# Low splits of the expert weights: from two engines in whole pieces to one engine in half pieces

## The reference

```
scores  = softmax(xt @ Wg.T)                   # 1024 tokens, 16 experts
combine = weights of the 4 experts of a token (from the 2 best groups of 4)
h       = silu(xt @ W1[e].T) * (xt @ W3[e].T)  # 176 wide
y       = sum over e of combine[:, e] * (h @ W2[e].T)
z       = silu(xt @ Ws1.T) * (xt @ Ws3.T) @ Ws2.T     # the shared expert, 352 wide
out     = x + y + z
```

## Time and profile before

| what | us |
|---|---|
| median of 3 runs (635.8 to 640.08) | 636.93 |
| the profiled execution | 642.02 |
| its span, first to last instruction | 640.6 |
| mean granted clock of TensorE | 0.961 of full |

### The profile page before, as it was taken

One profiled execution on the slowest core, in us unless ns is written; L12 is line 12 of the kernel. 1 busy time (PEld: TensorE's weight loads), 2 busy tenths in 40 slices (PEclk: granted clock), 3 DMA queues, 4 the chain that ended last, 5 costly groups with the idle time before them and its releaser, 6 DMA issues.

```text
span 640.6 us, 10499 instructions
## 1 busy us (share of the span) xinstructions
PE 569.4 (89%) x3751; PEld 470.4 (73%) x3751; DVE 391.3 (61%) x906; ACT 249.2 (39%) x515; POOL 211.5 (33%) x174
## 2 busy tenths in 40 slices
PE   6889999999999979999999998998889688999950
PEld 6668888898888978566566575676779477999940
DVE  3475765628356467866647655787656667555527
ACT  1334535535464351010312111236332477566630
POOL 3624540021000011322343332316165469444440
PEclk9889999999999999999999999999797898999985
DMA  8999904004030036996000000222061483334317
GB/s 246 265 237 226 202 14 165 1 1 180 12 113 2 1 116 222 336 331 223 1 0 1 1 1 1 111 118 76 17 231 67 119 283 91 108 112 128 115 37 293
DMA packets 25121, 76.93 MB, mean 120 GB/s; under 512 B 4839, under 2 KB 11631, under 8 KB 24432
## 3 DMA queue, kind: packets, MB, share of 16 engines
q1 hardware_dynamic: 19264, 62.33, 32.5%
q0 software_dynamic: 3792, 8.43, 3.7%
q10 hardware_dynamic: 2016, 5.50, 2.7%
HBM read 66.77 MB, written 28.48 MB: 149 GB/s over the span
## 4 chain that ended last, share of the span: by engine, by line
PE 58%; DVE 15%; issue 10%; DMA 7%; POOL 5%; ACT 3%; another core or an unknown queue 1%; SPq 1%; ACTq 0%; POOLq 0%; DVEq 0%
PE psum L684 8%; PE psum L702 6%; PE psum L853 5%; PE psum L553 5%; PE psum L618 5%; PE psum L605 5%; DMA sclB<-in_scl 5%; PE psum L566 4%; DVE tt L1254 3%; DVE Pb L1218 2%; PE psum L746 2%; POOL rows_of_experts L1631 2%; DMA yv<-parts_of_tokens 2%; PE psum L597 2%; PE psum L584 1%
## 5 line engine op out<-in xcount | busy, mean ns | idle before, releaser
L1254 DVE TENSOR_TENSOR tt<-psum,tab 128x512 f32<-128x512 f32 x96 | 60.8, 683 | 32.4 <-PE psum L684 31.9
L1603 POOL TENSOR_TENSOR rp<-tt,tt 128x512 f32<-128x512 f32 x24 | 30.7, 1278 | 106.1 <-DVE tt L1254 106.1
L553 PE MATMUL psum<-xTh,W 128*128 128x512 f32 x128 | 53.7, 419 | 8.4 <-DVE W L1154 6.6
L702 PE MATMUL psum<-rp,Mb 128*128 128x512 f32 x128 | 57.7, 595 | 0.3 <-DVE rp L1279 0.3
L853 PE MATMUL psum<-EW,xgh 128*128 x188 | 57.4, 347 | 0.4 <-issue 0.4
L1224 DVE TENSOR_TENSOR OTl<-psum,OTh 128x512 fp32r<-128x512 f32 x32 | 22.1, 692 | 53.9 <-ACT OTh L954 53.9
L553 PE MATMUL psum<-xTl,W 128*128 128x512 f32 x128 | 52.4, 410 | 0.0
L1637 POOL DMA_INDIRECT parts_of_tokens<-yb,xg x39 | 41.2, 1056 | 33.6 <-issue 26.7
L987 ACT ACTIVATE qP<-psum 128x512 f32<-128x512 f32 x16 | 9.6, 598 | 94.7 <-PE psum L702 94.7
L684 PE MATMUL psum<-xTh,Ah 128*128 128x512 f32 x96 | 41.9, 436 | 4.4 <-DVE ex_la L1334 2.3
L702 PEld LDWEIGHTS psum<-rp,Mb 128*128 128x128 f32 x128 | 23.7, 189 | 26.4 <-issue 25.7
(11 more groups left out here) (254 smaller groups left out, 1550.7 us busy)
## 6 DMA issues: line engine op xcount, KB each, us to landing
rows_of_experts<-in_empty SPq DMA_DIRECT2D x8, 2064.0 KB, 33.2
exr<-in_ex SPq DMA_DIRECT2D x9, 608.0 KB, 6.5
xg<-rows_of_experts SPq DMA_DIRECT2D x39, 129.0 KB
exr<-in_ex ACTq DMA_DIRECT2D x7, 608.0 KB, 4.7
raw<-in_codes SPq DMA_DIRECT2D x4, 1024.0 KB, 19.2
sclB<-in_scl SPq DMA_DIRECT2D x16, 256.0 KB, 11.4
yv<-parts_of_tokens SPq DMA_DIRECT2D x8, 512.0 KB, 7.3
raw<-in_codes SPq DMA_DIRECT2D x4, 512.0 KB, 16.7
```

Source lines behind the costliest of these rows:

```text
L553: mm = pe.matmul(ap, W[:, kt, m, 512 * hq + 128 * h:512 * hq + 128 * h + 128], xp[:, kt, 512 * g:512 * g + 512], start=(n == 0), stop=(n = ...
L702: mm = pe.matmul(ap, Mb[:, 4 * hp + 2 * kk + half_, :], rp[(j0 + kk) % 3][:, half_, :], start=(n == 0), stop=(n == 3))
L1254: return tt_(b3(tt[n][:, :], 64), b3(src, 64), tab[:, j % 3, n, :].unsqueeze(1).to_broadcast([128, 8, 64]), ALU.mult)
L1603: tt_(o[:, 0, :], tt[0][:, :], tt[1][:, :], ALU.subtract).then_inc(s_rp_lo, 1)
```

## The change

GpSimd keeps the low parts of experts 2 and 3 only. The low parts become entries of their own, `low`, in the order. Those of experts 0 to 3 stay where they were. Those of experts 4 to 15 move into steps 0 to 14 of the block order, on VectorE, in halves of 608 columns: the first half of a step's list stands between `block_turn` and `block_hidden`, the rest between `block_back` and `block_down`. The upper parts of experts 6 to 15, by ScalarE, are made in steps 1 to 12 but 5 and 10. The load of expert 9 moves from ahead of the first blocks into step 0, and those of 10 to 15 one step back.

```diff
-BY_POOL = (2, 3, 6, 8, 10, 12, 14)
+BY_POOL = (2, 3)
+LOWS = (((4, 0), (4, 1)), ((5, 0), (5, 1)), ((6, 0), (6, 1)), ((7, 0),), ((7, 1), (8, 0)), ((8, 1), (9, 0)),
+        ((9, 1),), ((10, 0), (10, 1)), ((11, 0),), ((11, 1), (12, 0)), ((12, 1), (13, 0)), ((13, 1),),
+        ((14, 0), (14, 1)), ((15, 0),), ((15, 1),))
+UPPERS = {1: 6, 2: 7, 3: 8, 4: 9, 6: 10, 7: 11, 8: 12, 9: 13, 11: 14, 12: 15}
...
-    yield from [("cross_turn", 6), ("cross_norm", 7, 0), ("cross_norm", 7, 1), ("expert", 0), ("cross_out", 5)]
+    yield from [("cross_turn", 6), ("cross_norm", 7, 0), ("cross_norm", 7, 1), ("expert", 0), ("low", 0), ("cross_out", 5)]
...
-    yield from [("norm_turn", 2, 5), ("copies", 4), ("mix", 0), ("expert", 1)]
+    yield from [("norm_turn", 2, 5), ("copies", 4), ("mix", 0), ("expert", 1), ("low", 1)]
...
-    yield from [("turn_low", 5), ("mix", 6), ("add_shared", 4), ("expert", 2), ("expert", 3)]
+    yield from [("turn_low", 5), ("mix", 6), ("add_shared", 4), ("expert", 2), ("low", 2), ("expert", 3), ("low", 3)]
...
-    yield [("expert_in", BEFORE)]
     yield [("block_turn", 0), ("block_turn", 1)]
     for s in range(NB + 2):
         step = []
         if s + AHEAD < NB:
             step += [("fetch", s + AHEAD)]
-        if BEFORE + 1 + s < NE:
-            step += [("expert_in", BEFORE + 1 + s)]
+        if BEFORE + s < NE:
+            step += [("expert_in", BEFORE + s)]
         if s + 2 < NB:
             step += [("block_turn", s + 2)]
+        lows = [("low", *low) for low in LOWS[s]] if s < len(LOWS) else []
+        step += lows[:1]
         if s < NB:
             step += [("block_hidden", s)]
         if 1 <= s <= NB:
             step += [("block_back", s - 1)]
+        step += lows[1:]
         if s >= 2:
             step += [("block_down", s - 2)]
-        if s + 6 < NE:
-            step += [("expert", s + 6)]
+        if s in UPPERS:
+            step += [("expert", UPPERS[s])]
         yield step
...
-            def expert(i):
+            def low(i, part=None):
                 if i in BY_POOL:
                     return
                 o = EW_E * EXPERT_AT[i]
                 ve.wait_ge(s_ex_hi, i + 1)
-                tt_(EW[:, o + 1216:o + 2432], exr[i][:, :], f32(EW[:, o:o + 1216]), ALU.subtract).then_inc(s_ex_dve, 1)
+                a, b = (0, 1216) if part is None else (608 * part, 608 * part + 608)
+                op = tt_(EW[:, o + 1216 + a:o + 1216 + b], exr[i][:, a:b], f32(EW[:, o + a:o + b]), ALU.subtract)
+                if part != 0:
+                    op.then_inc(s_ex_dve, 1)
...
-            def expert(i):
+            def low(i, part=None):
```

More of the change, by code:

```diff
@@ L1517, in vector_program @@
                     "cross_norm": cross_norm, "cross_out": cross_out, "pad": pad, "ready": ready, "route": route,
-                    "dispatch": dispatch, "table": table, "expert": expert, "mix": mix, "turn_low": turn_low,
+                    "dispatch": dispatch, "table": table, "low": low, "mix": mix, "turn_low": turn_low,
                     "add_shared": add_shared, "block_turn": block_turn,
@@ L1641, in gpsimd_program @@
                     "probs": probs, "bias": bias, "rotate": rotate, "split13": split13, "split2": split2,
-                    "expert": expert, "scatter": scatter, "block_down": block_down}
+                    "low": low, "scatter": scatter, "block_down": block_down}
             for name, *where in ORDER:
```

## The result

Ten runs of the changed kernel have a median of 631.77 us (627.17 to 633.42), ten of the kernel before 635.88 (633.11 to 640.08). The medians are 4.1 us apart, their quotient is 0.9935. The ratio that the comparison itself gives, with a 95% interval, is 0.9908 (0.9881 to 0.9935), which would be 5.9 us; it leaves out runs over 1.5% longer than the fastest of their kernel, of which there are none here. The forecast was 632.8 and 0.6% less. A later comparison of the same two kernels, with 6 and 17 runs, has medians 7.0 us apart and a ratio of 0.9873 (0.9842 to 0.9903).

The account below looks back on a forecast made before the run. The prediction saw TensorE losing 8.7 us over the first fifteen blocks, mainly to waits around VectorE's splits. Door 2.8 plus phase 1.3 gave 4.1 us off the median 636.93: 632.8 us, range 629.5 to 636.5.

Parts of the forecast that it names:

- Door, 2.8 us forecast: Ahead of block 0: without the low splits of experts 4 and 5 there, xgh(0) comes at 508.3 instead of 511.06; gain 2.8 us.
- I take no cost: Ahead of block 0: the first row blocks were taken to land in time; landing late would leave 0.2 us of the gain.
- row blocks land late: Rival ahead of block 0: late row blocks cut the gain to 1.3 us in all, 635.6 us; chance 0.08.
- the phase: Block 0 to block 15: 37.4 us against 38.7 before, a gain of 1.3 us.
- Pieces, 0.74 us from start to start: VectorE's 24 pieces of 608 columns in the phase: 0.74 us each from start to start, bounds 0.70 and 0.79.
- Pace and sum, 37.4 us: Steps of 2.67 us with two pieces, 2.26 with one and an upper split; all steps add up to 37.4 us.
- the loop: A chain through VectorE, TensorE and ScalarE spanning two steps: two neighbouring steps take at least 4.93 us.
- The clock: Rival: the slow clock, about 2 us, also falls in the new phase or is missing from timed runs before; 634.8 us; chance 0.20.
- What costs nothing: GpSimd's lost splits, its scatters, the later loads of experts 9 to 15 and ScalarE's upper splits were taken to add nothing.
- Scatters holding pieces (slower): Rival in the steps: pieces begun during a scatter wait for its end; 640 us at half, 647 at worst; chance 0.07.
- VectorE alone sets the pace (630.4 us): Rival in the phase: the loop never closes, pieces take 0.70 us, phase 35.0 us, gain 6.5 us, 630.4 us; chance 0.15.

Follow-up runs that it names:

- kind A: Executions, of either kernel, where GpSimd idles 3.3 to 3.7 us before its two splits, which begin 3.5 to 3.9 us ahead of the last gTh; five of fourteen profiles.
- kind B: Executions, of either kernel, where GpSimd's two splits begin right behind its last routing scatter, 2.1 to 2.2 us ahead of the last gTh; nine of fourteen profiles.
- the variant without the move: Changed kernel with the low splits of experts 4 and 5 put back ahead of block 0; median 631.54 us, ratio 0.9915 to the kernel before.
- the variant with the last piece earlier: Changed kernel with all pieces behind bth and the last piece in step 13 instead of 14; block 0 to block 15 35.02 us in one run.
- pieces behind bth: Changed kernel with every piece behind bth, none between xgl and bgg; median 628.92 us, ratio 0.9882 to the kernel before.
- fill spaced: Version "the filled door" with loads of experts 9 to 15 moved, none in steps 3 and 4; ratio 0.9856 to the kernel before.
- the door alone: Kernel before with only the low splits of experts 4 and 5 moved, whole, into steps 0 and 1; median 635.38 us against 636.49, ratio 0.9959.
- the filled door: Changed kernel with three pieces and expert 6's upper split between block_turn 1 and 2, the other pieces behind bth; median 627.54 us, ratio 0.9825 to the kernel before.
- the one of 533.48 above: A piece in the changed kernel with experts 6, 8, 10, 12, 14 given back to GpSimd in halves; that run's median 634.24 us, ratio 0.9945.

## Why the prediction was right

*Door, 2.8 us forecast.* Right in mechanism, and for the kind of execution that it was read from right in size too: in kind A the door is 2.8 us shorter (7.2 against 4.38), block 0 comes 4.4 us behind the gTh as the 509.9 of the prediction says, and "I take no cost" for the landing of the row blocks holds. What the prediction didn't know is that there is a kind B. There GpSimd's splits hold VectorE's for 3.7 us and not for 2.3, the clock is low behind it, and the row blocks land late; the first two make the gain larger, the third takes 0.8 us off it (the rival "row blocks land late" is in part what happened), and the door is worth 4.4 us. I had taken one execution's coincidence for the price. And I had set the move's gain at the door beside the phase's as if both were free of each other: the variant without the move shows that it costs the phase 1.5 us.

*Pieces, 0.74 us from start to start.* They are 0.70, each 0.785 long as the line between 512 and 1216 columns gave; the excess I added wasn't there.

*Pace and sum, 37.4 us.* It is 37.04, and two neighbouring steps take 4.90 us where the loop gave 4.93. From the xgl of step 0 to that of step 14 VectorE takes 34.0 us (506.46 to 540.50) where the sum had 34.5; the difference is the pieces' 0.04. Block 15's matmuls come 2.99 us after block 14's, and the variant with the last piece earlier shows that the piece is why.

*The clock.* In the changed kernel it is 1.00 throughout the phase, in both profiles; in the kernel before it falls at block 10 in all three. I had counted the fall as the old phase's cost, and the rival that it would come back, or be missing from the timed runs, has nothing for it. About 2 us was too much: the half clock lasts 3.4 us and costs at most 1.7. Gaps of TensorE of 1.5, 2.4 and 4.2 us stand ahead of falls here, but one of 2.8 us at the door of before and ones of 1.6 and 1.5 us in the variants "pieces behind bth" and "fill spaced" had none behind them, and the first fall of "the door alone" came with no gap of over 1.2 us ahead. So what brings a fall on stays open, and with it how much of the phase's gain is owed to its absence; by the bound of 1.7 us it can be all of the 1.7 us.

*What costs nothing.* The cover for the fetches of later row blocks, named there as slack, is thinner than I made it: with block 7 reached 1.8 us earlier than in the changed kernel (15.0 for 16.8, the filled door) block 10's row block is 2.4 us late.

*Scatters holding pieces (slower).* Refuted: 24 pieces beside the scatters average 785 ns. It is the scatters that take 1.58 us in place of 0.97 where a piece had just begun:

```profile
517.90 1.58 POOL L1646 DMA_INDIRECT parts_of_tokens<-yb,xg  x1 [1.61 <-ACT yb L1093]
520.20 0.97 POOL L1646 DMA_INDIRECT parts_of_tokens<-yb,xg  x1 [0.72 <-ACT yb L1093]
```

A piece began at 517.84, the next at 518.88. By the Trainium skill (SBUF — State Buffer, section Who interferes with whom) two instructions that read SBUF on both engines, VectorE's with two SBUF inputs, exclude each other, and whoever issues first blocks the other for the whole instruction. The traces here agree in all splits but the one of 533.48 above, with holds of up to 3.7 us. Its inference that a `tensor_tensor` leaves the making of descriptors alone doesn't agree: 0.6 us are added here, 1.0 by the whole splits of before.

*VectorE alone sets the pace (630.4 us).* Not in this order of instructions; with the pieces behind bth it does, to block 14.

The total of 4.1 us thus came out of a door read rightly for kind A and 1.6 too small for kind B, and a phase read 0.4 too small: 4.5 and 6.1 us by the traces. That the medians of the first comparison are 4.1 us apart is in part luck, since its own ratio says 5.9 and the later comparison 7.0 or more, over what either kind explains. The forecast was read from a profile of kind A, 642.02 us long, and carried over to timed runs with a median of 636.93. On two chips where before takes 641.7 and 644.0 us all four profiles are of kind A, on two where it takes 636.5 and 637.1 all eight are of kind B. So the timed runs of the result, at 635.9, were probably of kind B for the most part; that is argued, since a timed run doesn't tell its kind.

## What to carry to other kernels

Work that is handed from VectorE to GpSimd isn't free for VectorE when both read two SBUF operands: give it away only where VectorE has nothing of that kind, or keep it whole on VectorE in pieces short enough to stand in its gaps. Where a piece stands in a step matters as much as its length: put it behind the instruction that others wait for, not ahead, and look for the loop over two steps before summing one engine's work. A stretch that is made faster uncovers the next chain (here the ring of ten row buffers), so read how much slack the transfers have before counting on the whole gain. And a wait whose length depends on when one engine arrives at another's work has no single price: profile the kernel more than once, and compare only executions in which the engines meet in the same way.

## What the runs showed of the hardware

A VectorE split of 1.41 us that arrives while GpSimd runs the first of two of its own, back to back, waits for both: 5.03 and 5.10 us in two executions. It isn't let in between the two. Where it arrives 0.4 us into the second it takes 3.66 or 3.67 us, in three executions. I had expected the hold to be about constant from run to run; with the low clock behind the longer one it makes two kinds of door in the same kernel, 2.4 us apart.
